# A recommendation tower on one core: a third PSUM buffer for Gram units, subtractions cut in pieces, and the first ids spread by TensorE

## The chip, the cores and the metric

The kernel runs on one core of a Trainium2 chip. The metric is the device time of one execution in microseconds (us), the median of several executions. Engines are called as the profile calls them: PE is TensorE, PEld its weight loads, DVE VectorE, ACT ScalarE, POOL GpSimd, SP SyncE; SPq, ACTq and POOLq are their queues that issue DMAs.

## The reference

For a batch of 512 rows, 27 features are looked up in tables of 128 columns, all pairs of the 27 vectors of a row are multiplied, and a tower of three layers stands behind that:

```python
e = jnp.stack([tbl_0[ids[:, 0]], ..., tbl_26[ids[:, 26]]], axis=1)   # 512 x 27 x 128
dot = jnp.einsum('bnd,bmd->bnm', e, e)
z = dot.reshape(512, 27 * 27)[:, idx]           # the 351 pairs i < j
h = jnp.concatenate([z, dense_ctx], axis=1)     # 351 + 16 = 367
h = jnp.maximum(h @ W_top1 + b_top1, 0.0)       # 512 wide
h = jnp.maximum(h @ W_top2 + b_top2, 0.0)       # 256 wide
y = h @ W_top3
```

One table has 125,000 rows, eight have 12,500, the others 1,250 or 1,000.

## The kernel before, in words

The batch is cut into four tiles t = 0..3 of 128 rows. All vectors end up transposed in `embT` (embedding dimension on the partitions). They come there in two ways.

**Look-ups.** Eleven small tables (1,000 or 1,250 rows, so 8 or 10 chunks of 125) are loaded whole and looked up by TensorE, all 512 rows at once. For table k, DVE and ACT build one-hot matrices from `idrel` (the id minus the table row that begins a partition's part); ACT writes the table's high part `hi` in fp32r, DVE subtracts `lo = table - hi` (L555), and PE multiplies hi, then lo, with the one-hots into `acc[:, k % 2]` (L393, L399). ACT copies `acc` to `embT` (L603). The ids of table k must stand on every partition: for k >= 1 PE spreads them with one matmul (`spread_ids`, L375) of the ids `id_rows_r`, which ACT casts at L612, into a bank of `gram_ps`, and ACT makes `idrel` of it (L621). For k = 0 a DMA broadcasts them (`id_first`, L606), and DVE makes `idrel` (L539).

**Gathers.** Sixteen features in four groups of four are gathered by POOL with one indirect DMA for each feature and tile, 64 in all, in order of tile and group (L353). PE transposes a group (L367) and DVE or ACT (groups 0 and 2: DVE; 1 and 3: ACT) copies it to `embT` (L518). Six of the sixteen groups are transposed between look-ups (`AT_LOOKUP`), the others where `STEPS` says.

**Gram and tower.** After the look-ups all engines follow one list written out by hand, `STEPS`. A Gram unit (t, n), n = 0..3, is 8 matmuls into one of two halves of `gram_ps` (two banks each), L424; DVE and ACT copy its blocks to `pairs` (L511), four quadrants between them. PE may write unit u once unit u - 2 is copied. SP then moves rows of `pairs` with four DMAs for each tile (L323), PE computes `h1` (L438), ACT and DVE its relu, PE `h2` (L458), relu, and `y` (L469). For tiles 0 to 2 h1, h2 and y of tile t - 1 run after Gram units of tile t; at the end h1(2), one slot of h1(3), h2(2), the rest of h1(3), y(2), h2(3) and y(3) follow one another. `embT` of a whole tile must be there before its Gram unit 0.

Of the kernel before, what the change touches and what calls it, by code (L numbers as in the profile page):

```python
# [33 lines left out]
P = 128  # L34
# [42 lines left out]
def build_tower(nc, ids, ids_looked_up, dense_ctx_t, tables, W1, b1, W2, b2, W3, out):  # L77
# [50 lines left out]
    with ExitStack() as ctx:  # L128
# [35 lines left out]
        id_rows = sb("id_rows", [P, batch], I32)  # L164
        id_first = sb("id_first", [P, batch], I32)

# [13 lines left out]
        base_f_ready = sem("base_f_ready")  # L180
        id_first_loaded = sem("id_first_loaded")
        first_idrel_ready = sem("first_idrel_ready")
# [44 lines left out]
        for t in range(1, TILES - 1):  # L227
            STEPS += [("gram", t, 0)] + [("y", t - 2, None)] * (t >= 2) + [("gram", t, 1)] + tr(t + 1, [0])
            STEPS += [("gram", t, 2)] + tr(t + 1, [1]) + [("gram", t, 3), ("h1", t - 1, None)]
            STEPS += tr(t + 1, [2]) + [("h2", t - 1, None)] + tr(t + 1, [3])  # L230
        t = TILES - 1
        STEPS += [("gram", t, 0), ("y", t - 2, None)] + [("gram", t, u) for u in range(1, UNITS)]

# [31 lines left out]

        LAST = TILES - 1

        def h1_ps(t, n):
# [5 lines left out]
        def y_ps(t):  # L274
            return acc[:, 0, 3 * P + t:3 * P + t + 1] if t < LAST - 1 else gram_ps[:, 0, 0, t:t + 1]

# [81 lines left out]
        def _(pe):  # L358
# [11 lines left out]
            def spread_ids(k):  # L370

                if k >= 3:

                    pe.wait_ge(idrel_ready, k - 2)
                nc.tensor.matmul(spread_ps(k), pick[:, k:k + 1].broadcast_to([P, P]), id_rows_r[:, :],  # L375
                                 start=True, stop=True).then_inc(ids_spread, 1)
# [26 lines left out]
            def gram(t, n):  # L403
                if t == 0 and n == 0:

                    pe.wait_ge(vectors_out, NK)
                    pe.wait_ge(pads_zeroed, 1)
                if t == 1 and n == 0:

                    pe.wait_ge(vectors_out, NK + 1)  # L410

                if n == 0:
                    count = tr_index(t + 1, 0)
                    pe.wait_ge(embT_by[0], -(-count // 2))
                    pe.wait_ge(embT_by[1], count // 2)
                u = UNITS * t + n

                if u >= 2:
                    pe.wait_ge(pairs_by_dve, u - 1)
                    pe.wait_ge(pairs_by_act, u - 1)  # L420
                vectors = embT[:, t, :, :].rearrange("d p f -> d (p f)")
                for g in range(UNITG):
                    p0 = SG * (UNITG * n + g)
                    last = nc.tensor.matmul(gram_ps[0:ROWS, u % 2, g, 0:WIDTH], vectors[:, QUAD * p0:QUAD * p0 + ROWS],  # L424
                                            embT[:, t, p0:p0 + SG, 1:FEATS], start=True, stop=True)
                last.then_inc(gram_done, 1)

            def h1(t, slots):

                pe.wait_ge(pairs_by_dve, UNITS * (t + 1))  # L430
                pe.wait_ge(pairs_by_act, UNITS * (t + 1))
                pe.wait_ge(w1_loaded, 16)
                for n in range(H1C):
                    for a in slots:
                        if n == 0 and a == 0:

                            pe.wait_ge(rows_moved[t % 2], 16 * MOVES * (t // 2 + 1))
                        last = nc.tensor.matmul(h1_ps(t, n),  # L438
                                                w1_sb[:, a, P * n:P * (n + 1)], pairs[:, t % 2, a + MOVED_SLOTS, :],
                                                start=(a == UNMOVED), stop=(a == UNMOVED - 1))  # L440
                    if a == UNMOVED - 1:
                        last.then_inc(h1_done, 1)

            def h2(t):
                pe.wait_ge(weights_loaded, 16 * 4)
                if t == LAST:

                    pe.wait_ge(relu1_by_act, 2 * t)
                    pe.wait_ge(relu1_by_dve, 2 * t)
                if t < LAST - 1:  # L450

                    pe.wait_ge(relu1_by_act, 2 * t + 2)
                for m in range(H2C):
                    for c in range(H1C):
                        if m == 0:

                            pe.wait_ge(relu1_by_act if c < 2 else relu1_by_dve, 2 * t + c % 2 + 1)
                        last = nc.tensor.matmul(h2_ps(t, m), w2_sb[:, c, P * m:P * (m + 1)], h1T[:, t % 2, c, :],  # L458
                                                start=(c == 0), stop=(c == H1C - 1))
                    last.then_inc(h2_done, 1)  # L460
# [19 lines left out]
            pe.wait_ge(pick_ready, 1)  # L480
            pe.wait_ge(id_rows_ready, 1)
            spread_ids(1)
            for k in range(NK):
# [19 lines left out]
        def move_pairs(copy, t, n, s):  # L503

            view = gram_ps[QUAD * s:QUAD * s + FEATS - 1, (UNITS * t + n) % 2, :, :]
            c0 = (P // SG) * s + UNITG * n
# [16 lines left out]
        def _(dve):  # L523
# [6 lines left out]
            for n, ch in enumerate(SIZES):  # L530
# [5 lines left out]
            nc.vector.tensor_copy(pick[:, :], ident[:, 0:NK]).then_inc(pick_ready, 1)  # L536
            dve.wait_ge(id_first_loaded, 16)
            dve.wait_ge(base_f_ready, 1)
            nc.vector.tensor_scalar(idrel[0:ROWS_K, 0, 0:batch], id_first[0:ROWS_K, :], base_f[0:ROWS_K, own(0)], None,  # L539
                                    ALU.add).then_inc(first_idrel_ready, 1)  # L540
            for k in range(NK):
# [11 lines left out]
                for n, c in enumerate(parts(k)):  # L553
                    dve.wait_ge(hi_ready, parts_to(k) + n + 1)
                    nc.vector.tensor_tensor(lo[0:ROWS_K, b, c, :], table[0:ROWS_K, r, c, :], hi[0:ROWS_K, b, c, :],  # L555
                                            ALU.subtract).then_inc(lo_ready, 1)
                if k - 1 in AT_LOOKUP:
# [34 lines left out]
        def _(act):  # L592
# [12 lines left out]

            act.dma_start(id_first[:, :], ids_looked_up[0].partition_broadcast(P)).then_inc(id_first_loaded, 16)  # L606
            act.dma_start(id_rows[0:NK], ids_looked_up).then_inc(id_rows_loaded, 16)
            act.wait_ge(chunk_ready, 2)
            nc.scalar.activation(warm[:, :], chunk[:, 0:1], ACT.Square)
            act.wait_ge(id_rows_loaded, 16)  # L610
            act.wait_ge(id_rows_zeroed, 1)
            nc.scalar.copy(id_rows_r[0:NK, :], id_rows[0:NK]).then_inc(id_rows_ready, 1)  # L612
            act.wait_ge(base_f_ready, 1)
            for k in range(NK):
# [4 lines left out]
                if k >= 1:  # L619
                    act.wait_ge(ids_spread, k)  # L620
                    nc.scalar.activation(idrel[0:ROWS_K, b, 0:batch], spread_ps(k)[0:ROWS_K, :],  # L621
# [50 lines left out]
            act.wait_ge(y_done, LAST - 1)  # L672
            nc.scalar.copy(y_sb[:, 0:LAST - 1], acc[:, 0, 3 * P:3 * P + LAST - 1]).then_inc(y_copied, 1)

# [38 lines left out]
```

## Time and profile before

| what | us |
|---|---|
| median of 3 runs (120.3 to 121.19) | 120.91 |
| profiled execution, its own time | 120.88 |
| its span, first to last instruction | 119.1 |
| PE busy | 108.3 |
| DVE busy | 81.0 |
| ACT busy | 77.1 |
| POOL busy | 70.3 |

The span leaves out 1.8 us around the first and last instruction. Busy PE counts matmuls from start to modelled end, which overlap their successors. The granted clock of PE reads full in all forty slices. From the start to about 57 us the kernel does look-ups, then until 107 us Gram units with the tower of the tile before, then the tower of the last tiles.

### The profile page before, as it was taken

Reading aid. Unit: us, or ns where it says so; the run is one execution under the profiler, and the core shown is the slowest. Engines: PE = TensorE matmul, PEld = TensorE weight load, DVE = VectorE, ACT = ScalarE, POOL = GpSimd, SP = SyncE. Lnnn points to the kernel's source line nnn. Section 1 sums busy time; section 2 is a strip of 40 time slices with the busy share of each in tenths; the row PEclk is TensorE's granted clock in tenths of the full one; section 3 lists DMA queues with packets and bytes.
Section 4 is the critical chain, followed back from the end, with each engine's and each line's share of the span. In section 5 each row is a group of like instructions: output and inputs, shape, how many; then the busy total and the mean of one; then the engine's idle time right before and its main releaser. Section 6 shows DMA issues by size and latency. Waiting matters only on the chain.

```text
span 119.1 us, 2174 instructions
## 1 busy us (share of the span) xinstructions
PE 108.3 (91%) x728; PEld 97.2 (82%) x728; DVE 81.0 (68%) x253; ACT 77.1 (65%) x209; POOL 70.3 (59%) x72
## 2 busy tenths in 40 slices
PE   5089999999999999999799999979999779999991
PEld 4067888888878888888798999979999769999990
DVE  3199599995999996998488988341994506952121
ACT  3198599589979989983398869532786116970310
POOL 2377778878788777877776777767777300000000
PEclk9999999999999999999999999999999999999999
DMA  2999982885646779811221222222212200001000
GB/s 70 251 276 185 191 217 52 231 212 129 146 128 140 209 198 369 267 50 48 54 61 44 66 65 52 71 60 59 61 45 70 61 6 3 0 0 20 1 6 1
DMA packets 5805, 12.43 MB, mean 104 GB/s; under 512 B 2267, under 2 KB 3003, under 8 KB 5666
## 3 DMA queue, kind: packets, MB, share of 16 engines
q1 hardware_dynamic: 3580, 7.80, 23.9%
q0 software_dynamic: 2048, 4.20, 14.3%
q10 hardware_dynamic: 166, 0.28, 1.0%
q8 instruction: 6, 0.10, 0.3%
q14 instruction: 5, 0.04, 0.1%
HBM read 12.03 MB, written 0.00 MB: 101 GB/s over the span
## 4 chain that ended last, share of the span: by engine, by line
POOL 57%; issue 17%; PE 15%; DMA 6%; DVE 2%; POOLq 1%
POOL emb L353 57%; PE gram_ps L424 5%; DMA ids_sb<-in_ids 3%; PE gram_ps L438 3%; PE acc L438 3%; DMA emb<-in_tbl,ids_sb 2%; PE acc L458 2%; PE tr_ps L458 2%; DVE pairs L511 1%; POOLq L128 1%; PE gram_ps L469 1%; PE tr_ps L367 1%; DVE h2T L585 0%; PE acc L469 0%; DVE y_sb L589 0%
## 5 line engine op out<-in xcount | busy, mean ns | idle before, releaser
L353 POOL DMA_INDIRECT emb<-in_tbl,ids_sb x64 | 69.5, 1086 | 22.6 <-issue 19.2
L511 DVE COPY pairs<-gram_ps 26x56 f32<-26x56 f32 (+1 forms) x128 | 26.0, 203 | 12.1 <-PE gram_ps L424 10.3
L424 PE MATMUL gram_ps<-embT 128*122 128x104 f32 x256 | 29.9, 271 | 2.5 <-issue 1.4
L551 DVE TENSOR_SCALAR onehot<-idrel 125x512 fp32r<-125x512 f32 x81 | 29.1, 429 | 4.4 <-ACT idrel L621 4.3
L511 ACT COPY pairs<-gram_ps 26x56 f32<-26x56 f32 (+1 forms) x128 | 25.0, 195 | 10.9 <-PE gram_ps L424 9.4
L424 PEld LDWEIGHTS gram_ps<-embT 128*122 128x122 f32 x256 | 28.4, 187 | 3.6 <-issue 1.9
L393 PE MATMUL acc<-onehot,hi 125*128 125x512 f32 x92 | 25.0, 418 | 0.0
L399 PE MATMUL acc<-onehot,lo 125*128 125x512 f32 x92 | 23.4, 398 | 0.0
L399 PEld LDWEIGHTS acc<-onehot,lo 125*128 125x128 f32 x92 | 17.8, 194 | 4.3 <-DVE lo L555 0.4
L393 PEld LDWEIGHTS acc<-onehot,hi 125*128 125x128 f32 x92 | 17.8, 200 | 3.8 <-ACT hi L629 0.2
L603 ACT COPY embT<-acc 128x512 f32<-128x512 f32 (+2 forms) x12 | 12.2, 1035 | 7.8 <-PE acc L399 7.8
L555 DVE TENSOR_TENSOR lo<-table,hi 125x1024 fp32r<-125x1024 f32 (+2 forms) x13 | 14.0, 1087 | 0.0
L629 ACT CAST hi<-table 125x1024 fp32r<-125x1024 f32 (+2 forms) x13 | 12.4, 951 | 0.1
L438 PE MATMUL acc<-pairs,w_sb 128*128 128x128 f32 x96 | 11.3, 276 | 0.0
L438 PEld LDWEIGHTS acc<-pairs,w_sb 128*128 128x128 f32 x96 | 11.0, 192 | 0.0
L367 PE MATMUL tr_ps<-ident,emb 128*128 128x128 f32 x64 | 9.6, 273 | 0.7 <-DMA emb<-in_tbl,ids_sb 0.7
L367 PEld LDWEIGHTS tr_ps<-ident,emb 128*128 128x128 f32 x64 | 7.6, 142 | 1.8 <-DMA emb<-in_tbl,ids_sb 0.9
L636 ACT ACTIVATE near<-idrel,chunk 125x512 f32<-125x512 f32 x11 | 8.1, 735 | 0.0
L375 PE MATMUL gram_ps<-id_rows_r,pick 128*128 128x512 f32 x10 | 4.3, 432 | 3.8 <-ACT id_rows_r L612 3.8
L639 ACT ACTIVATE onehot<-near 125x512 fp32r<-125x512 f32 x11 | 7.0, 632 | 0.3
L621 ACT ACTIVATE idrel<-gram_ps,base_f 125x512 f32<-125x512 f32 x10 | 6.8, 684 | 0.0
L518 ACT COPY embT<-tr_ps 128x512 f32<-128x512 f32 x8 | 4.9, 608 | 2.9 <-PE tr_ps L367 2.9
(43 smaller groups left out, 53.7 us busy)
## 6 DMA issues: line engine op xcount, KB each, us to landing
table<-in_tbl SPq DMA_DIRECT2D x8, 480.0 KB
table<-in_tbl SPq DMA_DIRECT2D x2, 600.0 KB
emb<-in_tbl,ids_sb POOLq DMA_INDIRECT x64, 2.9
w_sb<-in_W SPq DMA_DIRECT2D x1, 1024.0 KB, 6.6
w_sb<-in_W SPq DMA_DIRECT2D x1, 512.0 KB, 8.3
table<-in_tbl SPq DMA_DIRECT2D x2, 240.0 KB
id_first<-in_ids_looked_up ACTq DMA_DIRECT2D x1, 256.0 KB, 4.8
pairs<-pairs SPq DMA_DIRECT2D x16, 15.0 KB
```

The lines of the kernel that those rows point to most:

```text
L353: pool.indirect_dma_start(emb[:, t % EMB_RING, gathered_features.index(f), :], None, tables[f], bass.IndirectOffsetOnAxis(ids_sb[:, t, f:f ...
L367: last = nc.tensor.transpose(tr_ps[:, n % 2, k, :], emb[:, t % EMB_RING, first + k, :], ident[:, :])
L393: nc.tensor.matmul(acc[:, b, 0:batch], hi[0:ROWS_K, b, c, :], one_hot(k, c), start=(c == 0), stop=False)
L399: last = nc.tensor.matmul(acc[:, b, 0:batch], lo[0:ROWS_K, b, c, :], one_hot(k, c), start=False, stop=(c == CHS[k] - 1))
L424: last = nc.tensor.matmul(gram_ps[0:ROWS, u % 2, g, 0:WIDTH], vectors[:, QUAD * p0:QUAD * p0 + ROWS], embT[:, t, p0:p0 + SG, 1:FEATS], sta ...
L438: last = nc.tensor.matmul(h1_ps(t, n), w1_sb[:, a, P * n:P * (n + 1)], pairs[:, t % 2, a + MOVED_SLOTS, :], start=(a == UNMOVED), stop=(a ...
L511: last = copy(pairs[QUAD * q:QUAD * q + FEATS - 1, t % 2, a:SLOTS, c0:c0 + UNITG], src.rearrange("r g a -> r a g"))
L551: nc.vector.tensor_scalar(one_hot(k, c), idrel[0:ROWS_K, b, 0:batch], float(c), None, ALU.is_equal).then_inc(onehot_by_dve, 1)
L555: nc.vector.tensor_tensor(lo[0:ROWS_K, b, c, :], table[0:ROWS_K, r, c, :], hi[0:ROWS_K, b, c, :], ALU.subtract).then_inc(lo_ready, 1)
L603: nc.scalar.copy(embT[:, tiles, :, LOOKED_UP[k]], src[:, tiles, :]).then_inc(vectors_out, 1)
L629: nc.scalar.copy(hi[0:ROWS_K, b, c, :], table[0:ROWS_K, r, c, :]).then_inc(hi_ready, 1)
L636: nc.scalar.activation(near[0:ROWS_K, 0:batch], idrel[0:ROWS_K, b, 0:batch], ACT.Square, bias=chunk[0:ROWS_K, own(k)]).then_inc(near_ready, 1)
```

## The change

1. A third buffer for Gram units. Unit 2 of each tile (`SPARE`) goes to the two banks of `acc` (tiles 0 to 2) or of `tr_ps` (tile 3); units 0, 1 and 3 alternate between the halves of `gram_ps`. New waits come with it: h1(0) and h1(1), which write `acc`, wait until unit 2 of the tile behind is copied; h2(2), which writes `tr_ps`, until unit (3, 2) is; unit (0, 2) until the last look-up has left `acc`. `y`'s column in `acc` moves to where no Gram unit writes.
2. DVE's subtractions are done in pieces of two chunks (256 columns) instead of 8 or 10 (in the first two look-ups 4), with one semaphore increment at the end of the part, as before.
3. The 256 KB broadcast `id_first` is gone. `id_rows` is the only DMA at the start of ACT's queue; DVE, not ACT, casts it; PE spreads the ids of table 0 as those of the others, and DVE makes `idrel` from PSUM.
4. In `STEPS`, transposes (2, 3) stand ahead of h2(0), where they stood behind it, and y(1) stands behind transposes (3, 3), where it stood behind Gram unit (3, 0).

```diff
@@
         for t in range(1, TILES - 1):
             STEPS += [("gram", t, 0)] + [("y", t - 2, None)] * (t >= 2) + [("gram", t, 1)] + tr(t + 1, [0])
             STEPS += [("gram", t, 2)] + tr(t + 1, [1]) + [("gram", t, 3), ("h1", t - 1, None)]
-            STEPS += tr(t + 1, [2]) + [("h2", t - 1, None)] + tr(t + 1, [3])
+            if t + 1 < TILES - 1:
+                STEPS += tr(t + 1, [2, 3]) + [("h2", t - 1, None)]
+            else:
+                STEPS += tr(t + 1, [2]) + [("h2", t - 1, None)] + tr(t + 1, [3]) + [("y", t - 1, None)]
         t = TILES - 1
-        STEPS += [("gram", t, 0), ("y", t - 2, None)] + [("gram", t, u) for u in range(1, UNITS)]
+        STEPS += [("gram", t, u) for u in range(UNITS)]
@@
+        SPARE = 2
+        Y_AT = 3 * P + WIDTH
+        def unit_buffer(t, n):
+            if n == SPARE:
+                return 2 if t < LAST else 3
+            return (t + (0, 1, None, 0)[n]) % 2
+        def unit_ps(t, n):
+            if n == SPARE:
+                return (acc[:, :, :].rearrange("p b (g c) -> p (b g) c", c=P) if t < LAST
+                        else tr_ps[:, :, :, :].rearrange("p b g c -> p (b g) c"))
+            return gram_ps[:, unit_buffer(t, n), :, :]
+        def copied_units(t, n):
+            for u in reversed(range(UNITS * t + n)):
+                if unit_buffer(u // UNITS, u % UNITS) == unit_buffer(t, n):
+                    return u + 1
+            return 0
@@ spread_ids(k)
+                if k == 2:
+                    pe.wait_ge(first_idrel_ready, 1)
@@ gram(t, n)
-                if t == 1 and n == 0:
+                if t == 0 and n == SPARE:
                     pe.wait_ge(vectors_out, NK + 1)
-                u = UNITS * t + n
-                if u >= 2:
-                    pe.wait_ge(pairs_by_dve, u - 1)
-                    pe.wait_ge(pairs_by_act, u - 1)
+                if copied_units(t, n) > 0:
+                    pe.wait_ge(pairs_by_dve, copied_units(t, n))
+                    pe.wait_ge(pairs_by_act, copied_units(t, n))
@@ h1(t, slots)
-                pe.wait_ge(pairs_by_dve, UNITS * (t + 1))
-                pe.wait_ge(pairs_by_act, UNITS * (t + 1))
+                copied = UNITS * (t + 1) + (SPARE + 1 if t < LAST - 1 else 0)
+                pe.wait_ge(pairs_by_dve, copied)
+                pe.wait_ge(pairs_by_act, copied)
@@ h2(t)
+                if t == LAST - 1:
+                    pe.wait_ge(pairs_by_dve, UNITS * LAST + SPARE + 1)
+                    pe.wait_ge(pairs_by_act, UNITS * LAST + SPARE + 1)
@@ tensor, ahead of the look-ups
+            spread_ids(0)
             spread_ids(1)
@@ vector
-            dve.wait_ge(id_first_loaded, 16)
+            dve.wait_ge(id_rows_loaded, 16)
+            dve.wait_ge(id_rows_zeroed, 1)
+            nc.vector.tensor_copy(id_rows_r[0:NK, :], id_rows[0:NK]).then_inc(id_rows_ready, 1)
             dve.wait_ge(base_f_ready, 1)
-            nc.vector.tensor_scalar(idrel[0:ROWS_K, 0, 0:batch], id_first[0:ROWS_K, :], base_f[0:ROWS_K, own(0)], None,
+            dve.wait_ge(ids_spread, 1)
+            nc.vector.tensor_scalar(idrel[0:ROWS_K, 0, 0:batch], spread_ps(0)[0:ROWS_K, :], base_f[0:ROWS_K, own(0)], None,
                                     ALU.add).then_inc(first_idrel_ready, 1)
@@
-                    nc.vector.tensor_tensor(lo[0:ROWS_K, b, c, :], table[0:ROWS_K, r, c, :], hi[0:ROWS_K, b, c, :],
-                                            ALU.subtract).then_inc(lo_ready, 1)
+                    for c0 in range(c.start, c.stop, 2):
+                        two = slice(c0, c0 + 2)
+                        last = nc.vector.tensor_tensor(lo[0:ROWS_K, b, two, :], table[0:ROWS_K, r, two, :],
+                                                       hi[0:ROWS_K, b, two, :], ALU.subtract)
+                    last.then_inc(lo_ready, 1)
@@ scalar
-            act.dma_start(id_first[:, :], ids_looked_up[0].partition_broadcast(P)).then_inc(id_first_loaded, 16)
-            act.wait_ge(id_rows_loaded, 16)
-            act.wait_ge(id_rows_zeroed, 1)
-            nc.scalar.copy(id_rows_r[0:NK, :], id_rows[0:NK]).then_inc(id_rows_ready, 1)
```

## Rows read from the trace of the kernel before

**Rows 1.** The page's part 4: shares of the chain that ended last, by engine.
```profile
POOL 57%; issue 17%; PE 15%; DMA 6%; DVE 2%; POOLq 1%
```

**Rows 2.** That chain in order of time: start us, us, what.
```profile
0.74 4.03 DMA ids_sb<-in_ids
...
5.05 1.13 POOL emb L353
...
55.34 0.94 POOL emb L353
...
92.78 2.53 DMA emb<-in_tbl,ids_sb
95.36 0.66 PE tr_ps L367 x4
...
96.73 1.92 PE gram_ps L424 x16
```

**Rows 3.** The timeline of PE, Gram and tower: start us, us, operation, count.
```profile
73.34 3.76 PE L438 MATMUL acc<-pairs,w_sb 128*128 128x128 f32 x32
...
79.16 0.60 PE L367 MATMUL tr_ps<-ident,emb 128*128 128x128 f32 x4
80.48 1.92 PE L424 MATMUL gram_ps<-embT 128*122 128x104 f32 x16 [0.72 <-issue]
...
92.67 1.95 PE L458 MATMUL acc<-h1T,w_sb 128*128 128x128 f32 x16
...
98.49 0.52 PE L469 MATMUL acc<-w_sb,h2T 128*128 128x1 f32 x4
98.88 5.70 PE L424 MATMUL gram_ps<-embT 128*122 128x104 f32 x48
104.42 3.76 PE L438 MATMUL acc<-pairs,w_sb 128*128 128x128 f32 x32
```

**Rows 4.** The timeline of all engines in the first look-ups: subtractions and gathers.
```profile
8.51 1.28 DVE L555 TENSOR_TENSOR lo<-table,hi 125x512 fp32r<-125x512 f32 x2
...
16.68 1.09 POOL L353 DMA_INDIRECT emb<-in_tbl,ids_sb  x1 [0.30 <-issue]
...
17.94 1.47 DVE L555 TENSOR_TENSOR lo<-table,hi 125x1280 fp32r<-125x1280 f32 x1
...
18.08 2.15 POOL L353 DMA_INDIRECT emb<-in_tbl,ids_sb  x1 [0.30 <-issue]
```

**Rows 5.** Groups of instructions by line and shape: busy us, mean ns of one.
```profile
L555 DVE TENSOR_TENSOR lo<-table,hi 125x1024 fp32r<-125x1024 f32 x7 | 8.5, 1210 | 0.0
...
L621 ACT ACTIVATE idrel<-gram_ps,base_f 125x512 f32<-125x512 f32 x10 | 6.8, 684 | 0.0
```

**Rows 6.** The timeline of all engines up to the first look-up.
```profile
5.57 0.49 DVE L539 TENSOR_SCALAR idrel<-id_first,base_f 125x512 f32<-125x512 int32 x1 [3.73 <-DMA id_first<-in_ids_looked_up]
5.75 0.62 ACT L612 CAST id_rows_r<-id_rows 11x512 fp32r<-11x512 int32 x1 [2.40 <-DMA id_rows<-in_ids_looked_up]
...
6.51 0.76 PE L375 MATMUL gram_ps<-id_rows_r,pick 128*128 128x512 f32 x1 [3.80 <-ACT id_rows_r L612]
...
7.07 3.69 PE L393 MATMUL acc<-onehot,hi 125*128 125x512 f32 x8
...
10.57 2.60 PE L399 MATMUL acc<-onehot,lo 125*128 125x512 f32 x8
```

**Rows 7.** The timeline of all engines in look-up 5, a table of ten chunks.
```profile
31.89 1.48 DVE L555 TENSOR_TENSOR lo<-table,hi 125x1280 fp32r<-125x1280 f32 x1
...
33.41 2.14 PEld L399 LDWEIGHTS acc<-onehot,lo 125*128 125x128 f32 x10 [0.43 <-DVE lo L555]
```

**Rows 8.** The timeline of DVE in the Gram units of tiles 0, 1 and 3.
```profile
65.53 3.53 DVE L511 COPY pairs<-gram_ps 26x48 f32<-26x48 f32 x16 [0.41 <-PE gram_ps L424]
...
71.66 1.71 DVE L511 COPY pairs<-gram_ps 26x48 f32<-26x48 f32 x8
...
104.62 1.72 DVE L511 COPY pairs<-gram_ps 26x48 f32<-26x48 f32 x8 [0.29 <-PE gram_ps L424]
```

More of the change, by code:

```diff
@@ L164, in build_tower @@
         id_rows = sb("id_rows", [P, batch], I32)
-        id_first = sb("id_first", [P, batch], I32)
         tr_ps = pb("tr_ps", [P, 2, 4, P])
@@ L180, in build_tower @@
         base_f_ready = sem("base_f_ready")
-        id_first_loaded = sem("id_first_loaded")
         first_idrel_ready = sem("first_idrel_ready")
@@ L274, in y_ps @@
         def y_ps(t):
-            return acc[:, 0, 3 * P + t:3 * P + t + 1] if t < LAST - 1 else gram_ps[:, 0, 0, t:t + 1]
+            return acc[:, 0, Y_AT + t:Y_AT + t + 1] if t < LAST - 1 else gram_ps[:, 0, 0, t:t + 1]
         def h1_read(t, n):
@@ L423, in gram @@
                     p0 = SG * (UNITG * n + g)
-                    last = nc.tensor.matmul(gram_ps[0:ROWS, u % 2, g, 0:WIDTH], vectors[:, QUAD * p0:QUAD * p0 + ROWS],
+                    last = nc.tensor.matmul(unit_ps(t, n)[0:ROWS, g, 0:WIDTH], vectors[:, QUAD * p0:QUAD * p0 + ROWS],
                                             embT[:, t, p0:p0 + SG, 1:FEATS], start=True, stop=True)
@@ L503, in move_pairs @@
         def move_pairs(copy, t, n, s):
-            view = gram_ps[QUAD * s:QUAD * s + FEATS - 1, (UNITS * t + n) % 2, :, :]
+            view = unit_ps(t, n)[QUAD * s:QUAD * s + FEATS - 1, :, :]
             c0 = (P // SG) * s + UNITG * n
@@ L619, in _ @@
                 if k >= 1:
-                    act.wait_ge(ids_spread, k)
+                    act.wait_ge(ids_spread, k + 1)
                     nc.scalar.activation(idrel[0:ROWS_K, b, 0:batch], spread_ps(k)[0:ROWS_K, :],
@@ L672, in _ @@
             act.wait_ge(y_done, LAST - 1)
-            nc.scalar.copy(y_sb[:, 0:LAST - 1], acc[:, 0, 3 * P:3 * P + LAST - 1]).then_inc(y_copied, 1)
+            nc.scalar.copy(y_sb[:, 0:LAST - 1], acc[:, 0, Y_AT:Y_AT + LAST - 1]).then_inc(y_copied, 1)
 def kernel(**inputs):
```

## The prediction

> **What bounds the kernel now.** I read the chain that ended last first. It is POOL's and its gaps' for three quarters of the span [rows 1]: once the ids have landed, POOL issues gather after gather without a pause, the last one lands 2.53 us after its start, at 95.31, and only then does PE make its last transposes, ACT copy them, and Gram unit (3, 0) start at 96.73 [rows 2]. From there to the end the chain is PE's. So all that PE saves ahead of 95.36 is worth nothing unless POOL saves too. But the timeline of PE shows how near the two are: h2(1) starts at 92.67; its sixteen matmuls take 1.95 us with the tail of the last one, 1.79 without [rows 3], so PE was free at 94.46, and has 0.9 us to spare. A saving of POOL alone would be worth 0.9 us at most. Both sides have to be summed up, and the later of the two sets the start of Gram unit (3, 0), G. Behind G comes a term of its own.
>
> **POOL's side.** The 33 gathers from 5.05 to 55.34 take 50.29 us, 1.52 us from start to start; the 30 from there to 92.78 take 37.44, 1.25 us each [rows 2]. An undisturbed gather in the look-ups has 1.09 + 0.30 = 1.39 us [rows 4]. The rest, 33 x 0.13 = 4.3 us, I lay to DVE's subtractions: a gather issued at 18.08, in a subtraction that runs from 17.94 to 19.41, takes 2.15 us instead of 1.09 and ends at 20.23, 0.82 us behind the end of the subtraction, as if it had been let in only then [rows 4]. The Trainium skill, page "SBUF — State Buffer", section "SBUF: two separate sides", describes such a block: DVE and GpSimd share a port pair as an exclusive lock for a whole instruction, and descriptors of a POOL-issued DMA wait for it.
>
> A gather that meets a piece waits for that piece alone. Gathers fall anywhere in a subtraction, so the chance to meet one stays and the mean wait shrinks with the length: with pieces a quarter as long about a quarter of 4.3 us stays, and 3.2 us go. Two or three more gathers then fall into the look-ups, at 1.39 instead of 1.25 us, 0.4 us back. Gain 2.8 us, with bounds of 0 (the pieces follow so closely that POOL isn't let in between) and 4.3.
>
> To this comes the start: POOL waits 4.03 us for the ids' DMA [rows 2], which shares the DMA engines with the 256 KB broadcast that goes. I take 0.5 us; the bounds are 0 and 1.5, since DMAs without such neighbours aren't shown at this place and the nearest, a gather, lands 2.53 us after its start [rows 2]. The last gather then lands at 95.31 - 2.8 - 0.5 = 92.0.
>
> **PE's side, term by term.**
>
> The start. Before, `id_first` landed at 5.57, and `idrel` was ready at 6.06; `id_rows`, second in ACT's queue, landed at 5.75; ACT's cast of it stood ahead of its first `hi`, and PE's first look-up started at 7.07 [rows 6]. After: `id_rows` (22 KB) is alone and first. Then a cast on DVE, 0.5 us (its conversion of the same width took 0.49), one matmul at the slow pace, 0.5 to 0.76, `idrel` out of PSUM, 0.68 as ACT's [rows 5, 6], and a one-hot, for which I take 0.4, an estimate from the 0.64 that a subtraction of the same width takes [rows 4]. That is 2.2 us behind the landing. If `id_rows` lands as the ids did, at 4.8, PE starts at 7.0; if it lands one microsecond earlier, at 6.0; if no earlier than before, at 5.75, at 7.95. Nearest is a small DMA with a clear queue, 4.2: start at 6.4. ACT's cast is no term, since `hi` is then long ready. Not all of it is kept: eight matmuls from 7.07 took 3.5 us, 0.44 each, and ten later ones 2.14, 0.21 to 0.24 each [rows 6, 7]. PE is at half pace at first, though the granted clock reads full, and if the pace rises at the same moment as before, half of an earlier start is lost. I take 0.4 us earlier, with bounds of 1.0 earlier and 0.9 later.
>
> The pieces. Two subtractions of four chunks take 1.28 us, one of eight 1.21 [rows 4, 5]: 0.07 us for each further instruction, so 0.21 us for a table of eight chunks, 0.28 for one of ten. In the nine to eleven look-ups PE is the one that is busy, and the single wait for a subtraction is that of look-up 5: 0.43 us, PE starting when the subtraction of 1.48 us ends [rows 7]. It becomes 0.28 longer, the other ones are hidden by DVE's waits for `idrel`. 0.3 us later; bounds 0 (if the earlier start of DVE covers it) and 1.0 (three more look-ups that lose 0.2 each).
>
> The third buffer ahead of G. DVE waited 0.41 us ahead of 65.53 for a unit that PE could only begin when another was copied [rows 8]. That and its like go. But then DVE is the bound, with 3.53 us for two units [rows 8], 1.75 each, against PE's 1.76 (96.73 to 98.49) [rows 2, 3]. And the new wait comes in: h1(0) started at 73.34 [rows 3], while DVE was at unit (1, 2), which is now in `acc`, until 71.66 + 1.71 = 73.37 [rows 8]. h1(0) must wait for exactly this. DVE can have this unit done some 0.3 us earlier at best, so the gain is 0.25, not what PE could run ahead. Behind the waiting h1 stand the transposes, h2 and the whole next tile. At h1(1) the same wait with no stall to recover costs 0.1. Net 0.15 us earlier, bounds 0.4 later and 0.5 earlier.
>
> Transposes (2, 3) ahead of h2(0). Before, they started at 79.16, and Gram unit (2, 0) at 80.48, after PE had stood idle for 0.72 us while ACT copied them [rows 3]. Now h2(0) hides that copy: 1.32 less the transposes' own 0.43 (0.60 without the tail of the last) gives 0.9 us. Their four gathers are the 45th to 48th; they come 16 gathers, 20 us, ahead of the last, so by 75.4, and PE wants them at 76 or later. If POOL did not speed up this is still enough. Bounds 0.6 and 0.9.
>
> Sum: 94.46 - 0.4 + 0.3 - 0.15 - 0.9 = 93.3. That is 1.3 us behind the last landing, 92.0. **PE is now the later side**, and gathers no longer bound. From the last transposes to G there are 1.37 us as before (95.36 to 96.73) [rows 2]; y(1), now in that gap, is hidden there. G is at 94.7 instead of 96.73, 2.0 us earlier.
>
> **Behind G.** y(1) took 98.88 - 98.49 = 0.39 us between two Gram units; the next three took 5.54 us to 104.42, against 5.28 at 1.76 each [rows 3]. With y(1) gone and unit (3, 2) in `tr_ps`, 0.65 us go. DVE's last copies started at 104.62 with a wait of 0.29 [rows 8], so they come earlier by about as much, and with them SP's moves, which h1(3) needs. h2(2)'s new wait is for copies finished microseconds before. Bounds 0.3 and 0.8.
>
> In all 2.0 + 0.65 = 2.7 us: a span of 116.4, and with the 1.78 us around it (120.88 less 119.1) 118.2. The profiled execution lies within 0.03 us of the median of the runs, so this is also the median I expect.
>
> **The rivals.**
>
> *The pieces don't let POOL in.* Then only the start helps it: landing at 94.8, G at 96.2, 0.5 us earlier, tail 0.65: 119.7. For it: one-hots run back to back as pieces would, and a gather beside them has 1.09 us, not 0.94, so POOL isn't free between them. Against: they cost it 0.15 us, and not a wait for a whole row of seven. The Trainium skill, same page and section, says that a DVE operation with two SBUF inputs holds the pair only against a GpSimd operation that reads SBUF; if gathers were not of that kind the subtractions would be no cause and this rival would hold. The row at 18.08 speaks against it. Chance 0.14.
>
> *The chain at the start is longer.* With `id_rows` landing at 5.75 PE starts 0.9 us later instead of 0.4 earlier: 119.5. Chance 0.10.
>
> *Slower: TensorE's pace.* PE now has two spreads at about 5, then a gap of more than a microsecond until the first one-hot. If the pace rises later for that, each matmul in between costs 0.44 instead of 0.23, so each microsecond of delay costs 0.48. Before, the eight `lo` matmuls from 10.57 took 2.60 [rows 6], which puts the rise near 12. The forecast's gain is used up when it comes after 17.5, in the second look-up; at 20 the kernel is at 122. For it: PE's busy stretch is now broken at its start. Against: the gap is shorter than the one ahead of 6.51. Chance 0.04.
>
> **How the numbers follow.** The forecast has 0.70, its own range being 117.2 to 119.2 by the bounds of the start (1.3 either way at most, half of that likely) and of the pieces. With the first rival the range must reach 119.8, and for a POOL and a start both better, 117.1. A measurement of this kernel tells a change of about 1% (1.2 us) from none. Faster by over 1% means below 119.7: nearly all of the forecast, most of the second rival and a third of the first, 0.82. Within 1% 0.13, slower 0.05.
>
> **What the profile will show.** Right: gathers in the look-ups at most about 1.35 us long; the last one landing near 92; the last transposes starting directly behind h2(1), with no wait for a DMA, or a short one; no idle 0.72 ahead of Gram unit (2, 0); y(1) in the gap ahead of unit (3, 0); a wait of PE for copies ahead of h1(0). The forecast is wrong if gathers beside pieces still take 1.5 us or more, if PE's first look-up begins after 7.5, or if PE waits for `lo` in more than two look-ups.

## The result, and the profile after

The changed kernel takes 117.34 us (median of 4 runs, 117.13 to 117.98), the one before 120.63 beside it; the ratio is 0.973, 95% interval 0.967 to 0.979. The profiled execution took 117.24 us with a span of 115.4, 3.7 us less than before. The forecast was 118.2, faster, and PE instead of POOL as what bounds.

The page's part 4, the chain that ended last by engine, answers to [rows 1]:

```profile
PE 70%; DVE 13%; DMA 6%; ACT 5%; issue 2%; SPq 2%
```

POOL is gone from the chain. The chain in order of time (start us, us, what), at its head and where the last gather stood [rows 2]:

```profile
3.12 6.44 DMA table<-in_tbl
9.58 0.62 ACT hi L659
...
13.36 1.79 DVE onehot L582 x5
...
16.58 1.68 DVE lo L588 x5
18.30 2.56 PE acc L423 x10
...
91.00 1.79 PE acc L485 x16
92.79 0.44 PE tr_ps L390 x4
93.23 0.39 PE acc L496 x4
93.62 0.33 issue
93.95 3.63 PE gram_ps L446 x32
```

The last transposes stand directly behind h2(1), y(1) behind them, and Gram unit (3, 0) starts at 93.95 instead of 96.73. But a part that I had not foreseen stands at the head: up to 18.3 us the chain runs over a table's DMA, ACT and DVE.

The timeline of the start (start us, us, engine, line, operation), against [rows 6]:

```profile
2.54 0.41 DVE L567 CAST id_rows_r<-id_rows 11x512 fp32r<-11x512 int32 x1 [0.70 <-DMA id_rows<-in_ids_looked_up]
2.97 1.11 POOL L376 DMA_INDIRECT emb<-in_tbl,ids_sb  x1 [1.33 <-DMA ids_sb<-in_ids]
3.98 0.75 DVE L570 TENSOR_SCALAR idrel<-gram_ps,base_f 125x512 f32<-125x512 f32 x1 [1.02 <-PE gram_ps L399]
4.53 0.62 ACT L659 CAST hi<-table 125x512 fp32r<-125x512 f32 x1 [1.66 <-DMA table<-in_tbl]
5.33 3.77 PE L417 MATMUL acc<-onehot,hi 125*128 125x512 f32 x8 [1.04 <-DVE onehot L582]
8.90 2.28 PE L423 MATMUL acc<-onehot,lo 125*128 125x512 f32 x8
9.58 0.62 ACT L659 CAST hi<-table 125x512 fp32r<-125x512 f32 x1 [1.50 <-DMA table<-in_tbl]
11.26 2.01 PE L417 MATMUL acc<-onehot,hi 125*128 125x512 f32 x8
```

`id_rows` landed at 2.54, 1.8 us after its issue, instead of 5.75; POOL starts 2.1 us earlier, look-up 0 1.7, look-up 1 2.0.

Gathers and subtractions on the timeline, where the long gathers of before were [rows 4], then the two long ones that are left with what DVE did then:

```profile
16.50 1.75 DVE L588 TENSOR_TENSOR lo<-table,hi 125x256 fp32r<-125x256 f32 x5
...
16.64 1.09 POOL L376 DMA_INDIRECT emb<-in_tbl,ids_sb  x1 [0.30 <-issue]
...
49.55 2.62 POOL L376 DMA_INDIRECT emb<-in_tbl,ids_sb  x1 [0.30 <-issue]
49.63 2.42 DVE L582 TENSOR_SCALAR onehot<-idrel 125x512 fp32r<-125x512 f32 x7
...
51.97 1.42 DVE L588 TENSOR_TENSOR lo<-table,hi 125x256 fp32r<-125x256 f32 x4
52.48 1.73 POOL L376 DMA_INDIRECT emb<-in_tbl,ids_sb  x1 [0.31 <-issue]
```

A gather inside a row of pieces takes 1.09 us, where one inside a whole subtraction took 2.15. The last gather starts at 88.23 (before 92.78) and lands some 2.5 us later, at 90.8, while PE is free for its transposes at 92.63. The timeline of PE, against [rows 3, 7]:

```profile
18.30 2.56 PE L423 MATMUL acc<-onehot,lo 125*128 125x512 f32 x10 [0.26 <-DVE lo L588]
...
32.34 2.56 PE L423 MATMUL acc<-onehot,lo 125*128 125x512 f32 x10 [0.33 <-DVE lo L588]
...
72.22 3.84 PE L461 MATMUL acc<-pairs,w_sb 128*128 128x128 f32 x32
75.89 1.04 PE L390 MATMUL tr_ps<-ident,emb 128*128 128x128 f32 x8
76.76 1.95 PE L485 MATMUL acc<-h1T,w_sb 128*128 128x128 f32 x16
78.55 1.85 PE L446 MATMUL gram_ps<-embT 128*122 128x104 f32 x16
...
100.83 3.75 PE L461 MATMUL acc<-pairs,w_sb 128*128 128x128 f32 x32
```

The 0.72 us ahead of Gram unit (2, 0) are gone. h1(0) starts at 72.22; DVE (below, against [rows 8]) copies unit (1, 2) until 72.16, so PE starts the moment that this copy ends:

```profile
70.45 1.71 DVE L539 COPY pairs<-acc 26x48 f32<-26x48 f32 x8
```

### The profile page after: what moved, and what is told of

It is laid out like the page before. It is cut to its first block, busy times and chain, and to the rows that moved or that the text cites. A ratio compares the mean times of both kernels' runs of the same rounds, so it can differ in the third digit from the quotient of the medians.

```text
span 115.4 us, 2207 instructions
## 1 busy us (share of the span) xinstructions
PE 108.6 (94%) x729; PEld 96.9 (84%) x729; DVE 83.7 (73%) x287; ACT 76.4 (66%) x208; POOL 67.8 (59%) x72
## 4 chain that ended last, share of the span: by engine, by line
PE 70%; DVE 13%; DMA 6%; ACT 5%; issue 2%; SPq 2%
PE gram_ps L446 15%; PE acc L423 14%; PE acc L461 10%; PE acc L417 10%; DMA table<-in_tbl 6%; DVE onehot L582 5%; PE tr_ps L390 5%; PE acc L485 5%; DVE pairs L539 4%; PE gram_ps L461 3%; PE acc L446 3%; DVE lo L588 3%; ACT embT L637 2%; PE tr_ps L485 2%; PE tr_ps L446 1%
## 5 line engine op out<-in xcount | busy, mean ns | idle before, releaser
L376 POOL DMA_INDIRECT emb<-in_tbl,ids_sb x64 | 67.0, 1047 | 20.5 <-issue 19.2
L539 DVE COPY pairs<-gram_ps 26x48 f32<-26x48 f32 (+1 forms) x96 | 19.5, 204 | 8.4 <-PE gram_ps L446 7.1
L539 ACT COPY pairs<-gram_ps 26x48 f32<-26x48 f32 (+1 forms) x96 | 18.7, 194 | 8.5 <-PE gram_ps L446 7.4
L446 PE MATMUL gram_ps<-embT 128*122 128x104 f32 x192 | 22.3, 270 | 1.2 <-ACT embT L637 0.7
L446 PEld LDWEIGHTS gram_ps<-embT 128*122 128x122 f32 x192 | 21.3, 187 | 1.7 <-ACT embT L637 0.9
L588 DVE TENSOR_TENSOR lo<-table,hi 125x256 fp32r<-125x256 f32 x46 | 16.3, 412 | 0.0
L614 DVE TENSOR_SCALAR h1T<-acc,b_sb 128x128 f32<-128x128 f32 x6 | 1.8, 347 | 5.9 <-PE acc L461 5.9
```

The costliest lines, as they stand in the source:

```text
L376: pool.indirect_dma_start(emb[:, t % EMB_RING, gathered_features.index(f), :], None, tables[f], bass.IndirectOffsetOnAxis(ids_sb[:, t, f:f ...
L446: last = nc.tensor.matmul(unit_ps(t, n)[0:ROWS, g, 0:WIDTH], vectors[:, QUAD * p0:QUAD * p0 + ROWS], embT[:, t, p0:p0 + SG, 1:FEATS], star ...
L539: last = copy(pairs[QUAD * q:QUAD * q + FEATS - 1, t % 2, a:SLOTS, c0:c0 + UNITG], src.rearrange("r g a -> r a g"))
L588: last = nc.vector.tensor_tensor(lo[0:ROWS_K, b, two, :], table[0:ROWS_K, r, two, :], hi[0:ROWS_K, b, two, :], ALU.subtract)
```

## The experiments

All but four of the kernels were timed on chips where the kernel before took 120.45 to 120.63 us. Their traces can be compared stretch by stretch, which tells more than the totals. I cut each at four starts of PE: look-up 1, Gram unit (0, 0), Gram unit (2, 0), Gram unit (3, 0), and end with the start of the last y:

```
                 to look-up 1   to (0,0)   to (2,0)   to (3,0)   to last y   last gather starts
before               13.24       44.30      22.94      16.25      19.63        92.78
after                11.26       45.46      21.83      15.40      19.04        88.23
e1 whole             11.32       44.82      21.82      15.39      19.04        88.98
e2 pieces only       13.82       45.20      22.93      15.30      19.62        88.28
e3 old start         13.07       45.25      21.82      15.39      19.03        89.89
e4 two buffers       12.22       45.28      22.04      15.23      19.30        85.51
e5 old order         12.12       45.25      22.70      15.47      19.37        86.05
e6 lo released       11.73       44.42      21.83      15.39      19.02        86.08
e7 start only        10.74       45.23      22.93      15.30      19.62        89.98
e12 both             10.51       44.56      21.81      15.40      19.02        86.24
```

The columns behind look-up 1 repeat to 0.1 us between kernels that are alike there (the look-ups to 0.2: 45.25 to 45.46). The first does not: with the same new start, look-up 1 begins anywhere from 10.7 to 12.2 us, and at 12.38 in e11 (below), a second trace of the changed kernel itself. All begin look-up 0 at 5.3; what differs is mainly when the matmuls of look-up 0 go from 0.44 us each to 0.23. Its eight `lo` matmuls in e7, all at the faster pace, and in e4, most at the slower:

```profile
8.65 2.02 PE L398 MATMUL acc<-onehot,lo 125*128 125x512 f32 x8
...
8.89 3.25 PE L418 MATMUL acc<-onehot,lo 125*128 125x512 f32 x8
```

So a difference of up to 1.5 us between two single traces ahead of look-up 1 says nothing of an edit. Single times of one kernel scatter by as much as 1.3 us (e4: 117.09 to 118.41).

**e1_whole.** Subtractions whole again.

```diff
-                    for c0 in range(c.start, c.stop, 2):
-                        two = slice(c0, c0 + 2)
-                        last = nc.vector.tensor_tensor(lo[0:ROWS_K, b, two, :], ...)
-                    last.then_inc(lo_ready, 1)
+                    nc.vector.tensor_tensor(lo[0:ROWS_K, b, c, :], ...).then_inc(lo_ready, 1)
```

> The changed kernel with its subtractions whole again. In the trace after, the last gather starts at 88.2 and PE is free for the last transposes at 92.6, having lost about 1 us in waits for lo in look-ups 2, 5 and 10. Theory (a subtraction keeps POOL out until it ends): gathers that meet one take 1.4 to 2.2 us, the last gather starts 3 to 4 us later, at 91 to 92, and lands at 93.5 to 94.7; PE, free at 91.8, waits for it, and the time is 118.2 to 119.4. Rival (the earlier start alone made POOL early, pieces do nothing for it): the last gather stays at 88 to 89, PE wins the 0.9 us of waits back, 116.5.

116.88 us, ratio 0.970 (0.967 to 0.973). My theory's number fell, and the rival's nearly came (116.5): the last gather starts at 88.98, 0.75 us later than with pieces and not 3 to 4. The mechanism is still there. Two of five long gathers of this trace:

```profile
30.94 1.77 POOL L376 DMA_INDIRECT emb<-in_tbl,ids_sb  x1 [0.30 <-issue]
...
34.41 1.89 POOL L376 DMA_INDIRECT emb<-in_tbl,ids_sb  x1 [0.30 <-issue]
```

They cost less here for two reasons: five gathers are over 1.2 us, by 2.5 us in all above 1.09, where before there were eight with 4.2; and the trace after has the two of 2.62 and 1.73 us instead, worth 2.2 us. Against e4, e5 and e6, which have the same pieces and no long gather, e1's last gather starts 2.9 to 3.5 us later: the pieces do for POOL what the theory said, and the trace after hides it. Above all POOL had got its 2.1 us from the start already. The last gather lands at about 91.5, PE is at its transposes at 92.03 and does not wait. So the pieces are not needed, and they cost PE 0.64 us between look-up 1 and Gram unit (0, 0) (45.46 against 44.82). By the times alone, 0.970 and 0.973, this is not resolved.

**e2_pieces_only.** The kernel before with the pieces and nothing else (the reverse of the diff above, on the kernel before).

> The kernel before with nothing but the pieces. Theory: the last gather starts 2.5 to 3.5 us earlier, but PE had 0.9 us to spare and loses 0.5 to 0.9 in longer waits for lo, so the time falls by 0 to 0.4 us only, 120.3 to 120.7, and PE no longer waits for the last gather. Rival (pieces don't let POOL in): last gather as before at 92.8, time 120.6 to 120.9, PE waits for it still.

120.75 us, ratio 1.001 (0.998 to 1.003). No gather is longer than 1.2 us, the last starts at 88.28, 4.5 us earlier, and nothing comes of it. The chain of this kernel where PE had waited for the DMA:

```profile
94.31 1.79 PE acc L458 x16
96.09 0.44 PE tr_ps L367 x4
96.53 0.72 issue
97.25 1.92 PE gram_ps L424 x16
```

The stretch up to Gram unit (3, 0) is 0.95 us shorter (16.25 to 15.30), the wait for the gather; the look-ups are 0.90 longer (44.30 to 45.20). 4.5 us of POOL bought 0.95, and the pieces took it back. As the theory said, just above its upper edge of 120.7.

**e3_old_start.** The changed kernel with the broadcast `id_first` and what goes with it again (part 3 of the change undone).

> The changed kernel with the 256 KB broadcast, the cast on ACT and idrel of table 0 from it again. Theory (the start is worth what the first look-up is earlier, since PE bounds): first look-up at 7.1 instead of 5.3, all of it kept to the end, 119.0 to 119.3. Rival (an earlier start is mostly lost to the half pace of the first matmuls or to the wait for the first one-hots): 117.6 to 118.2.

119.36 us, ratio 0.991 (0.987 to 0.994): 2.0 us above the changed kernel, and within 0.1 us of the theory's 119.0 to 119.3. Look-up 1 starts at 13.07, and all stretches behind are within 0.2 us of those of after.

**e7_start_only.** The kernel before with part 3 alone.

> The kernel before with nothing but the new start. Theory: ids land 2 us earlier and PE's first look-up starts 1.7 us earlier, so both sides move: last gather at 90.7 instead of 92.8, landing at 93.3, PE free at 92.6; time 2.0 us lower, 118.6 to 119.0. Rival (gathers then meet more of the whole subtractions and POOL keeps nothing): 119.8 or more.

117.88 us, ratio 0.977 (0.972 to 0.982). More than I expected: 2.6 us of the 3.3 come from the start alone. In its trace PE wins 2.5 us up to look-up 1, loses 0.93 in the look-ups, and wins the 0.95 of the gather wait, as POOL is 2.8 us earlier. Where the 0.93 go the timeline of look-ups 1 and 2 shows:

```profile
9.66 0.62 ACT L628 CAST hi<-table 125x512 fp32r<-125x512 f32 x1 [1.62 <-DMA table<-in_tbl]
...
12.72 0.66 ACT L620 ACTIVATE idrel<-gram_ps,base_f 125x512 f32<-125x512 f32 x1
...
13.41 3.26 DVE L554 TENSOR_SCALAR onehot<-idrel 125x512 fp32r<-125x512 f32 x9 [1.24 <-ACT idrel L620]
...
16.60 1.47 DVE L558 TENSOR_TENSOR lo<-table,hi 125x1280 fp32r<-125x1280 f32 x1
...
18.12 2.56 PE L398 MATMUL acc<-onehot,lo 125*128 125x512 f32 x10 [0.56 <-DVE lo L558]
```

ACT waits 1.62 us for table 1, with it `idrel` of table 2 comes late, DVE's nine one-hots behind that, then `lo`, then PE. Before, table 1 had landed ahead of ACT's need. In e7 and after this landing has become the limit that the start runs into: look-up 3 starts at 21.11 and 21.29 us there, though look-up 1 began at 10.74 and 11.26. The same start of look-up 3 in e1 and e6 has other grounds. In e1 (21.22) PE waits for a gather that was issued at 12.72 and landed at 20.77; in e6 (21.18) look-up 1 began at 11.73 and PE works from there on without a wait.

```profile
20.81 0.66 PE L390 MATMUL tr_ps<-ident,emb 128*128 128x128 f32 x4 [0.23 <-DMA emb<-in_tbl,ids_sb]
```

**e4_two_buffers.** The third buffer undone, with its waits.

```diff
-            if n == SPARE:
-                return 2 if t < LAST else 3
-            return (t + (0, 1, None, 0)[n]) % 2
+            return (UNITS * t + n) % 2
```

> The changed kernel with two halves of gram_ps alternating over all units, as before, and without the waits that came with the third. Theory (DVE's copies bound the Gram units anyway, so the third buffer is worth 0.1 to 0.3 us in tiles 0 and 1 and some 0.3 in tile 3): 117.6 to 117.9. Rival (the third buffer is what lets PE run ahead): 118.5 or more.

117.26 us, ratio 0.972 (0.969 to 0.976), no different from the changed kernel, and below the 117.6 to 117.9 of my theory. Stretch by stretch the third buffer gives 0.21 us in tiles 0 and 1, takes 0.17 in tile 2 (15.23 to 15.40), where h1(1) starts 0.09 later behind its unit, waiting for DVE's copy of unit (2, 2), and itself takes 0.08 longer, and gives 0.26 at the end: 0.3 in all, as the theory had it stretch by stretch, and less than the scatter of look-up 1. The rival, that PE could run ahead, is out.

**e5_old_order.** The old `STEPS`.

```diff
-            if t + 1 < TILES - 1:
-                STEPS += tr(t + 1, [2, 3]) + [("h2", t - 1, None)]
-            else:
-                STEPS += tr(t + 1, [2]) + [("h2", t - 1, None)] + tr(t + 1, [3]) + [("y", t - 1, None)]
+            STEPS += tr(t + 1, [2]) + [("h2", t - 1, None)] + tr(t + 1, [3])
-        STEPS += [("gram", t, u) for u in range(UNITS)]
+        STEPS += [("gram", t, 0), ("y", t - 2, None)] + [("gram", t, u) for u in range(1, UNITS)]
```

> The changed kernel with the old list of steps: transposes (2, 3) behind h2(0), y(1) behind Gram unit (3, 0). Theory: 0.7 to 0.9 us lost ahead of Gram unit (2, 0) and 0.4 at y(1), all of it kept to the end, 118.4 to 118.6. Rival (what follows had slack, the copies of DVE above all): 117.6 or less.

119.14 us, ratio 0.988 (0.983 to 0.992), 1.8 us above after and 0.5 above the theory's range. The stretches give 1.27 of it: 0.87 ahead of Gram unit (2, 0), 0.07, and 0.33 for y(1). The rest lies in the first column, 12.12 against 11.26, which the order of steps behind 60 us cannot have changed.

**e6_lo_released.** Each piece of `lo` releases its two chunks.

```diff
-                    last.then_inc(lo_ready, 1)
+                        nc.vector.tensor_tensor(lo[..., two, :], ...).then_inc(lo_ready, 1)
@@ look_up(k)
-                    for n, part in enumerate(parts(k)):
-                        if c == part.start:
-                            pe.wait_ge(lo_ready, parts_to(k) + n + 1)
+                    if c % 2 == 0:
+                        pe.wait_ge(lo_ready, sum(CHS[:k]) // 2 + c // 2 + 1)
```

> The changed kernel, but each piece of the subtraction releases its two chunks of lo to PE, where PE now waits for the last piece of a part. Theory (the pieces cost PE the waits for lo in look-ups 2, 5 and 10, about 1 us, and PE bounds): these waits go, PE is free for the last transposes 0.8 to 1.0 us earlier, while the last gather still lands about 91, 116.3 to 116.6. Rival (the time behind the waits is bound by ACT and DVE, which hand on one-hots and idrel no earlier): 117.1 to 117.4.

116.66 us, ratio 0.968 (0.964 to 0.973). PE's waits for `lo` are gone; in look-up 5 its matmuls follow one another:

```profile
29.36 2.54 PE L417 MATMUL acc<-onehot,hi 125*128 125x512 f32 x10
31.73 2.43 PE L422 MATMUL acc<-onehot,lo 125*128 125x512 f32 x10
```

The look-ups take 44.42 us instead of 45.46, as long as before the change to 0.1 us. The time is 0.7 us below the changed kernel's, as the theory said to 0.1 us; by the ratios alone (0.968 and 0.973, whose intervals overlap) the two are not told apart.

**e8_filled, e9_table1_halves, e10_both, e11_after_again.** Three kernels on top of e6, and the changed kernel again. In e8 PE works in the gap behind the first spreads; in e9 table 1 comes in two halves; e10 has both.

```diff
             spread_ids(1)
+            for _ in range(3):
+                nc.tensor.matmul(tr_ps[:, 1, 0, :], blank[:, :], blank[:, :], start=True, stop=True)
@@ load_table(k), e9 and e10
-                for n, c in enumerate(parts(k) if k == 0 else [slice(0, CHS[k])]):
-                    landed = first_part_loaded if k == 0 and n == 0 else table_loaded[r]
+                for n, c in enumerate(parts(k)):
+                    landed = first_part_loaded[k] if k < EARLY and n == 0 else table_loaded[r]
@@ scalar
-                    if k == 0 and n == 0:
-                        act.wait_ge(first_part_loaded, 16 * 2)
+                    if k < EARLY and n == 0:
+                        act.wait_ge(first_part_loaded[k], 16 * 2)
```

> The kernel that releases lo piece by piece (label e6), and behind the two first spreads three more matmuls of the blank tile, so that PE is busy in the gap from about 4.0 to 5.3 us. Look-up 0 starts at 5.3 us in all kernels with the new start, but look-up 1 at anything from 10.7 to 12.2 us, as PE comes to its full pace earlier or later in look-up 0. Theory (the gap between the spreads and the first one-hots keeps the pace at half for longer): full pace earlier, look-up 1 at 10.8 or before, look-up 3 at 20.4 instead of 21.2, 115.9 to 116.3. Rival (the full pace comes at a moment that this gap doesn't set, or ACT, behind table 1's landing at 8.3 to 9.6, sets look-up 2 anyway): 116.5 to 116.8.

> The same kernel as label e6, with table 1 loaded in two halves that have a semaphore each, as table 0 is, so that ACT can cast the first half about 1 us before the whole has landed. Theory (with the new start the landing of table 1 holds ACT, and through vectors(0) and idrel(2) the one-hots of look-up 2): ACT's wait for table 1 goes, idrel(2) comes 0.3 to 1 us earlier, look-up 3 starts 0 to 0.5 us earlier, 116.2 to 116.6. Rival (two more DMAs on SP's queue delay the tables behind, or PE's pace is what matters): 116.7 to 117.2.

> Both: the gap filled and table 1 in halves, on top of the release of lo by piece. If both theories hold, look-up 3 starts at 20.2 us or earlier and the time is 115.5 to 116.1; if neither, 116.5 to 117.0.

> The changed kernel as it is, once more and on the same chip as the three above. It tells how far a trace and a time of it repeat: 117.1 to 117.5 is expected. The start of look-up 1, 11.26 us in its first trace, should again lie between 10.7 and 12.3, and the two gathers of 2.6 and 1.7 us near 50 and 53 us will be there again if they belong to the kernel, and not if they belong to that execution.

They ran on one chip on which all kernels, the one before too, were far slower: 173.19, 174.38, 173.64 and 174.64 us against 157.31 of before (ratios 1.104, 1.107, 1.100 and 1.111, each to within 0.007). TensorE was held back there, as the windows of e11 show (stretch of core 0, busy us and count of PE, PEld, DVE, ACT, POOL, granted clock, DMA share, GB/s):

```profile
22.00:24.00 2.00, 2.00 (x10) 1.44 (x9) 1.38 (x4) 0.00 (x0) 1.69 (x2) 1.00 0.87 167
24.00:28.00 4.00, 2.12 (x6) 0.85 (x6) 0.00 (x0) 0.00 (x0) 3.02 (x4) 1.00 0.62 179
28.00:32.00 4.00, 1.60 (x3) 0.73 (x3) 0.00 (x0) 0.00 (x0) 2.85 (x4) 0.55 0.18 49
32.00:40.00 8.00, 0.00 (x0) 0.00 (x0) 0.00 (x0) 0.00 (x0) 6.17 (x7) 0.50 0.20 53
...
90.00:100.00 10.00, 10.00 (x48) 8.27 (x47) 9.30 (x27) 7.58 (x11) 2.03 (x2) 1.00 0.47 135
```

So the totals say nothing on fills and halves. They do say that on this chip the four kernels with the new start are 10 to 11% slower than the one before, of which no trace was taken there (its executions had a mean granted clock of 0.88, theirs 0.82 to 0.84). Whether the change causes it, and which part, stays open.

The head of these traces can be read, as the clock is full there and the matmuls follow one another: look-up 1 starts at 10.06 us in e8 and 10.18 in e10, and at 10.90 and 12.38 in e9 and e11, which have no fill. Look-up 3 starts at 20.60 in e8 and 20.34 in e9, so either edit alone can get below 21.1: e9 has no fill, and its ACT casts table 1 at 7.59 without a wait, while e8's still waits 1.24 us for the table, until 8.92. These are single traces; in e10 (20.62) ACT stood idle for 3.0 us ahead of its copy at 18.03, so that this start says nothing. And e11, the changed kernel, has no gather above 1.2 us, where its first trace has the two of 2.62 and 1.73. But its look-ups of that place fell into the time of the held TensorE, so whether they belong to the kernel stays open.

**e12_both_again.** The kernel of e10 once more.

> The kernel of label e10 (lo released by piece, the gap behind the first spreads filled, table 1 in halves) once more, as its first run fell on a chip that held TensorE back for some 60 us and said nothing on the total. In the first 15 us of that run look-up 1 began at 10.2 and look-up 2 at 14.5 us, against 11.3 and 15.5 in the changed kernel. Theory: this head start of 1 us is kept, look-up 3 begins at 20.2 us or earlier instead of 21.2, 115.5 to 116.1. Rival (ACT and DVE, not PE, set the pace of look-ups 2 to 5, so the lead is lost there): 116.5 to 116.8, as label e6. If TensorE is held back on this chip too, the times are again 150 us or more for both kernels and only the first look-ups can be read.

115.70 us, ratio 0.960 (0.956 to 0.963), 4.75 us below the 120.45 of before beside it and clear of the changed kernel's interval, as the theory said. It is the best of all. The start of its timeline:

```profile
4.02 1.48 PE L512 MATMUL tr_ps<-blank 128*128 128x128 f32 x6
...
5.32 3.29 PE L418 MATMUL acc<-onehot,hi 125*128 125x512 f32 x8
...
7.55 0.61 ACT L660 CAST hi<-table 125x512 fp32r<-125x512 f32 x1
...
10.51 1.98 PE L418 MATMUL acc<-onehot,hi 125*128 125x512 f32 x8
...
20.08 2.08 PE L418 MATMUL acc<-onehot,hi 125*128 125x512 f32 x8
```

The first eight matmuls take 3.3 us instead of 3.8, ACT finds table 1 there at 7.55 without a wait, and look-up 3 begins at 20.08, 1.0 us before the earliest without these edits (21.11 in e7). Which share of the time is the fill's and which the halves' stays open: alone they ran only on the chip that held TensorE back.

## Why the prediction was right, and where it was off

**What bounds.** Right. PE no longer waits for the last gather: 92.63 against a landing at 90.8, 1.8 us apart where I had 1.3.

**POOL's side.** Right in kind, too small, and worth less than its place in the argument. The last gather starts 4.55 us earlier; I had 3.3; in e4, e5 and e6, without the two long gathers, it is 6.7 to 7.3. The ids' DMA gave 2.1 us where I took 0.5 and bounded it by 1.5. The pieces let POOL in, which e2 shows by itself (4.5 us against my 2.8 and its bound of 4.3), so the first rival is out. The Trainium skill ("SBUF — State Buffer", "SBUF: two separate sides") says that a DVE operation with two SBUF inputs blocks only a GpSimd operation that reads SBUF. This case doesn't speak against that: the profile names `ids_sb`, a tile in SBUF, among what each gather reads. But e1 shows that no piece was needed once the start was there. I had costed the two sides each as a sum of all edits, and never asked which edit alone would already put POOL ahead.

**The start.** The mis-sized term, and nearly the whole of the error. I had 0.4 us earlier, with 1.0 as the bound; measured are 1.74 at look-up 0, 1.98 at look-up 1 and 1.41 at look-up 3. The step that failed is "nearest is a small DMA with a clear queue, 4.2": `id_rows` landed at 2.54. The landing of the ids at 4.77 was itself the product of the 256 KB that go, and a row taken beside it was no measure for what is left: with the broadcast back (e3) the first gather starts at 4.93 us again, with the new start alone (e7) at 2.95. What I added behind the landing (2.2 us) was 2.8. Of the loss that I feared from the half pace nothing shows in this pair, 1.74 us having become 1.98 by look-up 1; but that is luck of the two traces, since without a fill the gain at look-up 1 is anything from 0.9 us (e11) to 2.5 (e7). What I had not seen is the next thing to be late, table 1's landing. The chain of after runs through it, and the way from look-up 1 to look-up 3 grew from 9.46 to 10.03 us: of the 1.6 us that the start gave beyond my 0.4, 0.6 were lost there.

**The pieces.** 0.3 us later, bounds to 1.0: measured 0.64 (e1 against after) and 0.90 (e2 against before). The price of a further instruction was right (1.42 us for four pieces against 1.21); the waits are in look-ups 2 and 10 too, not in 5 alone. The one in look-up 2 comes with the earlier start: e7 has it without pieces (0.56 us), e2 and e3, with pieces and the old start, have not.

**The third buffer.** 0.15 us ahead of G: measured 0.04 (0.21 less 0.17), and the wait of h1(0) for DVE's unit (1, 2) is in the trace as written. (DVE's 3.53 us for two units are 1.77 each, not 1.75; the argument stands.) **The order.** 0.9 us: 0.87. **Behind G.** 0.65 us: 0.59.

**The sum.** 2.7 us against 3.3 by the medians and 3.6 in the pair of profiled executions. In that pair the stretches are -1.98, +1.16, -1.11, -0.85 and -0.59, together 3.37 of the 3.7 by which the span shrank; the rest lies behind the last y. The time, 117.34 us, is near the lower end of my range, which I had kept for a POOL and a start both better, and both were. That the sum came out so near is in part luck: the start gave 1.98 us where I had 0.4, and the look-ups took back 1.16 where I had 0.3.

**The signs.** By the letter two of my signs of a wrong forecast came. A gather beside pieces still took 1.73 us, and one beside one-hots 2.62; and PE waits for `lo` in three look-ups, not in at most two (0.26, 0.33 and some 0.16 us). The mechanism is not touched, as POOL had 1.8 us in hand and the waits are small, but as limits they were set too tightly.

The slower rival, a later full pace of PE, did not come in the way described: the pace rose during look-up 0 in all traces of the new start.

## What to carry to other kernels

When two engines are nearly level ahead of a join, cost each edit alone against both, because one edit may already decide the join and leave another as pure cost: here the start did POOL's part too, and the pieces cost PE 0.6 us for nothing. A DMA's time to landing next to a large one is no price for the same DMA without it. When work is cut in pieces for the sake of one engine, release the pieces one by one to the next (the look-ups went from 45.46 to 44.42 us here).

## What was not expected of the hardware

- A 22 KB DMA landed 1.8 us after its issue when it stood first in its queue, and some 4.6 us after it behind a 256 KB broadcast (1.18 to 5.75). The ids, 54 KB on another queue and issued at 0.74 in both, landed 2.1 us earlier without the broadcast.
- A gather usually gets in between DVE instructions that follow one another every 0.35 us (it then takes 1.04 to 1.13 us), but in two traces, after and e3, one gather lasted 2.62 us, to just behind the end of a row of seven one-hots, and the next 1.73, until 0.82 us behind the last of four pieces. The one-hots took 2.42 us instead of 2.54, as if nobody had come between them. The traces of e2, e4, e5, e6 and e12, with the same pieces, have neither. The cause is open.
- TensorE starts at half pace with the granted clock at 1.00, and when it reaches full pace differs from trace to trace: with the same work ahead of it look-up 1 begins at 10.7 to 12.4 us (eight traces). In the three traces with three matmuls of zeros in the gap of 1.0 us ahead of look-up 0 it begins at 10.1 to 10.5.
- On one of the chips, TensorE's granted clock was 1.00 until 28 us, after busy look-ups from 5 us on, and from 32 to 88 it was 0.50, its level of 1.2 GHz, but for some 4 us from 52 on (0.93). Single matmuls came up to 3.5 us apart in that time, and the first gaps come before the clock falls: from 24 to 28 us six matmuls in 4 us with the clock still at 1.00. DVE and ACT waited. Elsewhere the clock reads 1.00, 2.4 GHz, throughout. A kernel that is 3% faster elsewhere was 11% slower there.
